# All dense f32r products as pairs of 64-row matmuls, spread one turn at a time between the score stages

## The reference

```python
xn = _layernorm(x)                                   # x: (16, 1024, 256), eps 1e-5
Q, K, V = xn @ Wq.T + bq, xn @ Wk.T + bk, xn @ Wv.T + bv   # 16 heads of 16
Q, K = _rope(Q, pos), _rope(K, pos)
scores = where(causal, einsum('bhqd,bhkd->bhqk', Q, K) / 4, -1e9)
attn = einsum('bhqk,bhkd->bhqd', softmax(scores), V)
attn_out = concat(attn) @ Wo.T + bo
h = square(relu(xn @ W_fc.T))                        # 256 -> 1024
y = h @ W_proj.T                                     # 1024 -> 256
spikes = 5 steps of a leaky integrate-and-fire neuron driven by y, counted / 5
out = x + attn_out + spikes
```

## Time and profile before

| | before |
|---|---|
| median of 3 runs | 2248.03 us |
| the runs | 2238.79, 2248.03, 2248.32 us |
| span of the profiled execution | 2243.2 us |
| the profiled execution's own time | not listed apart; its span is already above the lowest run |
| granted TensorE clock, mean | 0.987 |
| PE, PEld busy | 96%, 63% |
| DVE, ACT, POOL busy | 64%, 64%, 49% |

### The profile page before, as it was taken

One profiled execution on the slowest core, in us unless ns is written; L12 is line 12 of the kernel. 1 busy time (PEld: TensorE's weight loads), 2 busy tenths in 40 slices (PEclk: granted clock), 3 DMA queues, 4 the chain that ended last, 5 costly groups with the idle time before them and its releaser, 6 DMA issues.

```text
span 2243.2 us, 48570 instructions
## 1 busy us (share of the span) xinstructions
PE 2156.2 (96%) x16276; PEld 1406.2 (63%) x16276; DVE 1441.2 (64%) x2134; ACT 1437.5 (64%) x1673; POOL 1097.5 (49%) x1074
## 2 busy tenths in 40 slices
PE   3799999999999999999999999999999999989995
PEld 2656666666666666666666666666666666656653
DVE  5646566766757676566757667676676757646543
ACT  2376766667576675766667576665757667666663
POOL 4455454554645455453545545455464545535431
PEclk9899999999999999999999999999999999999998
DMA  3352544536345353644536354453634635345433
GB/s 137 110 175 88 157 130 115 182 87 197 101 127 168 97 184 88 173 115 132 174 84 192 101 143 144 113 185 84 188 106 120 181 91 181 92 133 155 109 97 94
DMA packets 169785, 298.89 MB, mean 133 GB/s; under 512 B 25089, under 2 KB 114945, under 8 KB 157185
## 3 DMA queue, kind: packets, MB, share of 16 engines
q1 hardware_dynamic: 169600, 296.10, 45.8%
HBM read 174.89 MB, written 103.28 MB: 124 GB/s over the span
## 4 chain that ended last, share of the span: by engine, by line
PE 83%; DVE 6%; ACT 4%; issue 4%; DMA 1%; POOL 1%; SPq 0%; ACTq 0%; DVEq 0%; POOLq 0%
PE pair L1068 33%; PE pair L1264 20%; PE pair L1228 15%; PE pair L1247 15%; ACT probs L708 2%; DVE count L928 2%; DVE stats L792 1%; ACT xT_hi L673 1%; PE pair L1155 1%; DVE h_sq L913 1%; DVE denom L852 1%; ACT h_sq L699 1%; PE pair L1080 1%; DVE numer L951 1%; POOL rot L599 0%
## 5 line engine op out<-in xcount | busy, mean ns | idle before, releaser
L708 ACT ACTIVATE probs<-pair 128x1024 f32<-128x1024 f32 x1152 | 1117.9, 1026 | 490.3 <-PE pair L1247 482.8
L617 POOL TENSOR_SCALAR_AFFINE_SELECT probs<-probs 128x512 f32<-128x512 f32 x512 | 375.0, 752 | 484.8 <-ACT probs L708 484.8
L609 POOL TENSOR_TENSOR h_lo<-h_sq,h_hi 128x512 fp32r<-128x512 f32 x256 | 383.9, 1500 | 437.4 <-DVE h_hi L915 436.9
L1264 PE MATMUL pair<-probs,v_sb 128*17 128x512 f32 (+3 forms) x6144 | 546.9, 489 | 6.1 <-DVE numer L951 5.2
L1247 PE MATMUL pair<-q_ring,k_ring 64*128 64x512 f32 (+3 forms) x3072 | 440.7, 381 | 16.8 <-ACT probs L708 13.7
L913 DVE TENSOR_TENSOR h_sq<-h_sq 128x512 f32<-128x512 f32 x256 | 201.3, 786 | 352.2 <-ACT h_sq L699 352.2
L1247 PEld LDWEIGHTS pair<-q_ring,k_ring 64*128 64x128 f32 x3072 | 227.3, 185 | 272.6 <-ACT probs L708 172.7
L1264 PEld LDWEIGHTS pair<-probs,v_sb 128*17 128x17 f32 x6144 | 152.3, 97 | 297.7 <-issue 264.1
L928 DVE SCALAR_TENSOR_TENSOR count<-y_sb,count 128x512 bf16<-128x512 f32 x256 | 294.1, 1149 | 6.8
L1228 PE MATMUL pair<-wproj_hi,h_hi 128*128 128x256 f32 x1024 | 293.0, 286 | 1.3 <-POOL h_lo L609 1.3
L1228 PE MATMUL pair<-wproj_lo,h_hi 128*128 128x256 f32 x1024 | 289.6, 283 | 0.0
(11 more groups left out here) (89 smaller groups left out, 2592.4 us busy)
## 6 DMA issues: line engine op xcount, KB each, us to landing
q_ring<-qk_dram SPq DMA_DIRECT2D x384, 128.0 KB
k_ring<-qk_dram SPq DMA_DIRECT2D x384, 128.0 KB
qk_dram<-planes SPq DMA_DIRECT2D x64, 512.0 KB, 2.8
qk_dram<-rot_b SPq DMA_DIRECT2D x64, 512.0 KB, 3.9
xn<-in_x SPq DMA_DIRECT2D x17, 1024.0 KB, 7.0
rs<-in_x SPq DMA_DIRECT2D x64, 256.0 KB, 2.7
acc_dram<-rs SPq DMA_DIRECT2D x64, 256.0 KB, 4.5
attn<-numer SPq DMA_DIRECT2D x256, 64.0 KB, 2.3
```

The lines of the kernel that those rows point to most:

```text
L609: pool.tensor_tensor(h_lo[i % HB][:, :], h_sq[i % HB][:, :], h_hi[i % HB][:, :].bitcast(F32), ALU.subtract).then_inc(h_lo_done, 1)
L617: ins = pool.affine_select(view, view, [[0, 4], [1, P]], ALU.is_ge, 0.0, base=0, channel_multiplier=-1)
L708: act.activation(probs[BUFFER[n]][:, 2 * pr:2 * pr + 2, :], pair[m % NSLOT][:, :, :], ACT.Exp, scale=SCALE).then_inc(exp_done, 1)
L1264: ins = pe.matmul(pv_bank[32 * i:32 * i + VW, q0 - g * G:G], v_sb[:, kt, 4 * quad + i, :], probs[BUFFER[n]][:, i, at:at + width(kt, g)], s ...
```

## The change

1. **Pairs.** Each dense product is issued as 64-row matmuls in pairs, one on each row half. A product is thus done in two *turns*: in turn 0 it uses the rows of one half, in turn 1 those of the other. `query_key` pairs its even and odd halves (6 pairs of 512 columns a turn); `values` pairs two token groups, or a group with a contraction carried over from the interval before; `expand` and `contract` are paired with each other (12 pairs of 256 columns a turn): the expansion of item i runs beside the contraction of item i-2.
2. **Items.** An item is now 256 features of 256 tokens; there are 16 as before. Expansion has two PSUM banks, y has one, Q/K uses the two expansion banks, and so do the values. Y is copied four times an interval instead of two times two banks.
3. **Places.** A step has five places. Score stages stand at 0, 1, 3 and 4; at 2 stand the weigh run, norms, transposes and output. After each score stage the tables `VALUES_AT`, `QK_AT` and `MLP_AT` put at most one turn, or none. An interval has 6 value turns, 8 Q/K turns and 30 MLP turns. ACT, DVE and POOL follow the same places.
4. **Moves.** Transposes go from steps 1 and 2 to 2 and 3, output from steps 3-6 to 4-7, norms from step 7 to step 8 (into `pair0`, so the stage of step 8, place 3 waits for DVE's last read, `shift_used`). On SP `store_out` goes to steps 5-8 and `store_planes` from 4-7 to 5-8, each behind what stood at step 5: `load_ring(b, d, 2, ...)`. `gather(b, 0)` goes from step 6 to 8. Spikes are issued one DVE instruction a place.

```diff
-V_AT = {0: (0, 1)}
-V_EARLY = {1: (2, 3)}
-T_AT = {1: (0, 1, 2), 2: (3,)}
-QK_AT = {2: ((0, 0), (0, 1)), 3: ((1, 0), (1, 1)), 4: ((2, 0), (2, 1)), 5: ((3, 0), (3, 1))}
-O_AT = {3: 0, 4: 1, 5: 2, 6: 3}
-NORM_AT = 7
+PLACES = 5
+VALUES_AT = {(0, 0): (0, 0), (0, 3): (0, 1), (0, 4): (1, 0), (1, 0): (1, 1), (1, 3): (2, 0), (1, 4): (2, 1)}
+TAKE_V_AT = {(0, 3): (0,), (1, 0): (1,), (1, 4): (2, 3)}
+T_AT = {2: (0, 1, 2), 3: (3,)}
+QK_AT = {(2, 4): (0, 0), (3, 0): (0, 1), (3, 4): (1, 0), (4, 0): (1, 1), (4, 4): (2, 0), (5, 0): (2, 1),
+         (5, 4): (3, 0), (6, 0): (3, 1)}
+ROTATE_AT = {at: u for at, (u, turn) in QK_AT.items() if turn}
+PLANE_AT = {(4, 0): 0, (5, 0): 1, (6, 0): 2, (7, 0): 3}
+LOW_QK_AT = {(4, 3): 0, (5, 3): 1, (6, 3): 2, (7, 3): 3}
+O_AT = {4: 0, 5: 1, 6: 2, 7: 3}
+NORM_AT = 8
+MLP_AT = {(6, 4): (0,), (7, 0): (1,), (8, 0): (2,), (8, 2): (3, 4), (9, 0): (5,), (9, 3): (6,), (9, 4): (7,),
+          (10, 0): (8,), (10, 1): (9,), (10, 4): (10,), (11, 0): (11,), (11, 3): (12,), (11, 4): (13,),
+          (12, 0): (14,), (12, 3): (15,), (12, 4): (16,), (13, 0): (17,), (13, 3): (18,), (13, 4): (19,),
+          (14, 0): (20,), (14, 3): (21,), (15, 0): (22,), (15, 3): (23,), (15, 4): (24,),
+          (16, 0): (25,), (16, 3): (26,), (16, 4): (27,), (17, 0): (28,), (17, 3): (29,)}
+Y_AT = {(10, 1): 0, (13, 0): 1, (16, 0): 2}
...
-        fc_bank, proj_bank = bank_a, (bank_b, bank_c)
+        proj_bank, fc_bank = pair[2][:, 1, :], (pair[3][:, 0, :], pair[3][:, 1, :])
+        qk_bank = fc_bank
+        norm_bank, first_norm_bank = pair[0][:, 0, :], pair[1][:, 0, :]
...
 # SP
-                    if more and n == 4:
-                        store_planes(nb, nd, 0)
-                    if last and n in (4, 5):
-                        store_out(b - 1, d - 1, n - 4)
-                    if more and n == 5:
-                        store_planes(nb, nd, 1)
                     if att and n == 5:
                         load_ring(b, d, 2, b * 2 * NUNIT + 2 * NU)
+                    if last and n in (5, 6, 7, 8):
+                        store_out(b - 1, d - 1, n - 5)
+                    if more and n in (5, 6, 7, 8):
+                        store_planes(nb, nd, n - 5)
...
 # PE
+            def query_key(nb, u, turn, tb):
+                if turn:
+                    pe.wait_ge(qk_turn, nb * 4 + u + 1)
+                elif u == 0:
+                    pe.wait_ge(xT_lo_done, tb * 4 + 3)
+                else:
+                    pe.wait_ge(rot_done, nb * 4 + u)
...
+                for n, (w, x, k) in enumerate(terms):
+                    for eo in range(2):
+                        rows = half_rows(eo + turn)
...
+            def expand_part(i, turn, n):
+                g, f, k, term = i // ITEMS_OF_GROUP, 2 * (i % ITEMS_OF_GROUP) + n // 6, n // 3 % KD, n % 3
+                rows, m, a = half_rows(i + turn), slice(f * P, (f + 1) * P), n // 6
+                w, x = ((wfc_hi, xT_hi), (wfc_lo, xT_hi), (wfc_hi, xT_lo))[term]
+                return pe.matmul(fc_bank[i % 2][:, a * T2:(a + 1) * T2], w[rows, k, m], x[rows, k, g * T2:(g + 1) * T2], ...)
...
+            def await_contract(item, i, turn, out=None, copied=None):
+                if turn:
+                    pe.wait_ge(proj_turn, item + i + 1)
+                    return
...
+                if copied is not None and i % ITEMS_OF_GROUP == 0:
+                    pe.wait_ge(y_copied, copied + i // ITEMS_OF_GROUP)
+                pe.wait_ge(h_lo_done, item + i + 1)
...
+            def expand_and_contract(nb, item, i, j, turn, out, copied, first, final):
+                await_expand(nb, item, i, turn, first, final)
+                await_contract(item, j, turn, out, copied)
+                for n in range(PART):
+                    h, y = expand_part(i, turn, n), contract_part(j, turn, n)
+                h.then_inc(fc_ps if turn else fc_turn, 1)
+                y.then_inc(proj_done if turn else proj_turn, 1)
...
+                for at in ((n, place) for n in range(NSTEP) for place in range(PLACES)):
+                    if att and place != 2:
+                        scores(b, 2 * n + place // 3, place % 3, last, more)
+                    if att and place == 2 and n in RUN_AT:
+                        run(b, RUN_AT[n], last)
...
+                    if more and at in QK_AT:
+                        query_key(nb, *QK_AT[at], tb)
+                    for t in turns.get(at, ()):
+                        mlp_turn(b, nb, item, t, last, first, final, again)
```

More of the change, by code:

```diff
@@ L111 @@
[L111 to L116, removed]
@@ new lines, in interval @@
+                    if last and place == 2 and n in O_AT:
+                        finish(b - 1, O_AT[n])
+                    if more and at in LOW_QK_AT:
+                        low_qk(nb, LOW_QK_AT[at])
+                    if more and at == (NORM_AT, 2):
+                        bound(nb, first_norm_bank if first else norm_bank)
+                        if first:
+                            replicate_bias()
+                    for i in expanded.get(at, ()) if more or final else ():
+                        activate_h(item, i)
@@ L980, in interval @@
-                    if more and n in SPIKES_NEXT:
-                        a, part = SPIKES_NEXT[n]
-                        spikes(half_of(b, 0, first, final, again), (nb * 2 + again) * 2 + a, a, range(3 * part, 3 * part + 3),
-                               nb * 4 + a + 1)
+                    if final and at in SPIKES_FINAL:
+                        a = SPIKES_FINAL[at]
+                        for s in range(STEPS + 1):
+                            spikes(half_of(b, 1, first, final, again), B * 4 + a, a, s)
@@ L1000, in interval @@
-                    for u, eo in QK_AT.get(n, ()) if more else ():
-                        rotate(nb, u, eo, items_before(b, again) if att else None)
-                    if last and n in O_AT:
-                        finish(b - 1, O_AT[n], final_bank if final else o_bank)
-                    if more and n == NORM_AT and not first:
-                        bound(nb, norm_bank)
-                    if (more or final) and n in expand_early:
-                        activate_h(item, expand_early[n])
@@ L1017, in interval @@
-                    if more and not first and n == Y1_AT or final and n == Y_FINAL_AT:
-                        take_y(half_of(b, 1, first, final, again), item + NFC - 1)
-                    if first and n == 12:
+                    if first and at == (12, 4):
                         whole_bias()
@@ new lines, in mlp_turn @@
+            def mlp_turn(b, nb, item, t, last, first, final, again):
+                i0, end, k, turn = NFT if final else 0, NFT if first else NFC, t // 2, t % 2
+                if k == 0:
+                    if first and turn == 0:
+                        pe.wait_ge(w_lo[2], 1)
+                    expand_together(nb, item, i0, turn, first, final)
+                elif i0 + k + 1 < end:
+                    if first and t == 2:
+                        pe.wait_ge(w_lo[3], 1)
+                    out = (b - 1) * 4 + 4 if last and k == 1 else None
+                    copied = copies_before(b, again) - (NTG // 2 if final else 0) if not first else 0 if k > 1 else None
+                    expand_and_contract(nb, item, i0 + k + 1, i0 + k - 1, turn, out, copied, first, final)
+                else:
+                    contract_alone(item, i0 + k - 1, turn)
@@ L1311, in interval @@
[L1311 to L1317 removed]
+                    if more and at == (NORM_AT, 2):
+                        if att:
+                            pe.wait_ge(exp_done, b * 2 * NUNIT + NORM_PAIR - NSLOT + 1)
+                        norms(nb, first_norm_bank if first else norm_bank)
@@ new lines, in interval @@
+                    for m in T_AT.get(n, ()) if place == 2 and (more or final) else ():
+                        transpose(b, tb, m, att, again)
+                    if last and place == 2 and n in O_AT:
+                        output(b - 1, O_AT[n])
+                    if att and at in values_at:
+                        m, turn = values_at[at]
+                        if carried and m < CARRIED:
+                            values_and_contract(b, m, turn, again)
+                        else:
+                            values_together(b, m, turn, again)
```

550 lines of the change are left out of this document (271 added, 279 removed).

## The result

The changed kernel takes 2436.28 us (median of 4 runs, 2427.05 to 2439.31), the kernel before 2244.84 us beside it (4 runs): ratio 1.085, 95% interval 1.082 to 1.089. I had forecast 2313 us, and 2370 as the upper end: slower was right, the size was off by almost a factor of three.

A forecast was written before the change was run, and what follows sets the result against it. PE was taken as the bound, busy 133.2 of 133.5 us an interval. 133.5 - 6.9 (tiling changes) + 10.9 (waits) = 137.5 us; +60 us for 15 intervals and +5 for the first on 2248 gave 2313 us, range 2205 to 2370.

The forecast's parts named there:

- turn 1 close behind turn 0: PE wait for turn 0's last matmul before loading, 0.13 us each, 11 times: 1.4 us an interval; bounds 0 and 0.23.
- Changes of tiling: Tiling changes on PE fall from 73 to 38 an interval, about 0.20 us each: 6.9 us removed.
- Streaming: Matmul streaming unchanged: pairs of 256 columns 0.12 us apart, a turn 1.43 us, a Q/K turn 1.37.
- Step 5, place 4: PE waits 3.6 us at a Q/K turn for a rotation whose store lands late behind 13 ring DMAs.
- Step 6, place 4: PE waits 1.9 us at the first MLP turn for the rotation, store landing and odd half.
- waits do not hold PE: Rival: long landing waits and gaps between turns covered, 4.0 us of waits remain, 130.6 us an interval, 2210 us; chance 0.26.
- The issue bound: Rival: dense matmul issue makes pairs 5% slower, 2.6 us an interval more, 2352 us; chance 0.09.
- Step 2, place 4: PE waits 1.2 us at a Q/K turn for high and low parts of three blocks after the transposes.
- Steps 8 and 9, place 0: PE waits 1.0 us each for exp, as three score stages follow each other with two PSUM pairs.
- The h chain just covered: ReLU to remainder gets over 5 us of cover, taken as no wait; if not, 1 to 3 us more.
- The first interval, +5: The first interval, without score stages as cover, takes 5 us more.
- The changes remain: Rival: row halves with other operands still empty the array, so the 6.9 us stay, 2417 us; chance 0.05.

The follow-up runs named there:

- e2: e1 with the four bias adds on POOL moved from iteration 13 place 4 to iteration 14 place 4; 2321.48 us, ratio 1.037.
- e3: e2 with every dense product on the whole 128-row array again, same places and queue orders; 2481.17 us, ratio 1.107.
- b1: The kernel before, with SP's third-part ring loads put ahead of the first Q/K plane's store, old tilings kept; 2342.46 us, ratio 1.044.
- e1: The changed kernel with SP's third-part ring loads put back behind the first and second Q/K plane stores; 2365.02 us, ratio 1.056.
- e5: e2 with four MLP turns moved: the first two, the fifth, and turn 23 to ahead of a weigh run; 2311.48 us, ratio 1.031.
- e7: e5 with exp on half its columns, middle spike comparisons on 64 of 512, masks on one head of four; 2285.55 us, ratio 1.019.
- c1: e2 with both turns of each MLP product together, 15 blocks instead of 30 spread turns; 2457.54 us, ratio 1.095.
- e6: e5 with the second MLP turn moved to iteration 7 place 4 and the third to iteration 8 place 2; 2287.36 us, ratio 1.020.

## Why the prediction was wrong, point by point

My interval was 133.5 - 6.9 + 10.9 = 137.5 us; it is 145.8, 8.3 more. The 1.4 us for turn 1 close behind turn 0, which I had booked as a wait, is an open load, and the account above counts it as PE's own time. So I had own time fall by 5.5 us (6.9 - 1.4) and waits rise by 9.5. At full clock own time fell by 3.0 (2.5 us missing), the slow clock added 3.0, and stands rose by 12.2 (2.7 more; the weigh run of step 15 alone is 2.85). That is 8.2 us.

- **Changes of tiling, 6.9 us removed: the count right, the gain too large by 2.5 us.** 612 groups are 38 an interval, as counted. But PE's own time falls by 3.0 us only (133.1 to 130.1, read in e2, where the clock is full). By kind: scores -3.0, MLP and values together -0.8, output with its own change +0.6. The failed step is to take the whole "about 0.20 us" of a change, the step at the boundary and the open load behind it, as gone with the change. e3 bears the 0.20 out only where nothing else holds the load; on the average it is 0.15, because in the pairs' version a load stays open where a turn waits on a semaphore. "I am fairly sure of this term" stood over the one that carried the rival of a gain.
- **Streaming: right a pair (0.12 us), wrong a turn.** 1.48 against 1.43, Q/K 1.47 against 1.37, for the open first load. Over the 44 turns of an interval it is 2.3 us (64.7 of own time against 62.4), nearly all of the 2.5 missing above. The issue bound is out: pairs hold 0.12 through whole turns. The rule of the Trainium skill that I cited, "TensorE: Matmul & The Clock Gate", section "Wait — 56ns, not 53.3ns?", would make a pair 0.124 us. The trace shows 0.117 to 0.121, so it does not bound this kernel; whether hardware decoding was off, as the rule asks, no run shows.
- **Step 5, place 4: mechanism and place right, 3.6 us against 4.8.** The landing took 5.0 us and not 3.9. b1 shows that I had also read its cover wrongly: even the old kernel stands with this order.
- **Step 6, place 4: 1.9 us against none**, since the longer wait ahead of it gave DVE its time; it is there (1.1 us) once that one is gone (e1, e2). I had added two waits that lie one behind the other on the same chain. The landing in this chain has a second waiter that I had not walked, ACT's ReLU (iteration 8, place 1: about 1 us in e1, e2, e5 and e7).
- **Step 2, place 4: 1.2 against 1.17. Steps 8 and 9, place 0: 1.0 each against 1.05 and 1.07. Step 10, place 4: 0.5 against 0.49. Step 1, place 3: 0.3 against 0.44.** The short chains, walked from rows, came out almost to the digit.
- **Turn 1 close behind turn 0:** with a score stage between, it shows only as the open load, 0.18 us a product (0.34 + 1.51 against 0.23 + 1.44) where I had 0.13; without one it is 0.30 to 0.34 us (c1), above my upper bound of 0.23.
- **"The h chain just covered": true of h, false of what shares its queue.** The missing step is the weigh run of step 15, 2.85 us for a mask that stood on POOL behind the bias adds and a remainder of h. I had walked the places that had changed, and this run had not; what had changed was how soon PE came to it.
- **The clock: not in my sum at all.** Behind the stands of 4.8 and 2.7 us it was granted at half for some microseconds; together 3.0 us an interval (133.1 against 130.1 of own time), a quarter of the 12.2 us that an interval grew. e1 and e2 take away the stands, and the slow turns go with them, but for one in twelve intervals.
- **The first interval, +5: it is +17.6.** A stand of 6.4 us at the fourth Q/K turn is in it, the slow clock (0.93 in that interval), and turns that follow each other directly, each with the wait of c1.

Of the rivals, "waits do not hold PE" was wrong at its root. Its 2210 us counted on 126.6 us of own time and 4.0 of waits; with 130.1 the same waits make an interval of 134.1 us, a little longer than the old one. "The changes remain" (2417) has the nearest number for another reason.

In the order of their size, shown by an experiment each: SP's order (67 us, e1, and 98 in the old kernel, b1), POOL's order (44, e2), the spread's short waits (37, e5 and e6). Against them stands what the pairs save in these places, 160 us (e3 against e2), but compared with the old places only 3.0 us an interval. What stays open: how the remaining 44 us of e6 divide among the single chains; I did not try to remove the wait for `xT_lo` or the one for the landing behind ACT's ReLU, and the start and the end of the run were not studied.

## What to carry to other kernels

When PE's order is tightened, walk every queue again, not only the places that moved: a store behind 13 loads on SP, a mask behind bias adds on POOL, or a bank shared with an output product cost more here than the tiling changes gave back. Price a removed change as the difference between two kernels that differ in nothing else; the rows around one change also hold the open load, which a semaphore keeps open just as well. Count a stand of PE of some microseconds with the slow clock behind it. And where a wait is put down to exp, look at what the engine did just before: here it was a DMA's landing.

## What the runs showed of the hardware

- The granted clock fell to 0.50 in the turn right behind a stand of 4.84 us, and was back in the next turn, some 3 us later; behind one of 2.7 us in the weigh run it fell only 1.4 us after PE had gone on. In b1 the same happened behind 3.18 us with whole-row matmuls. Behind a stand of 1.86 us it fell in one of twelve intervals of e2, and behind 1.7 to 2.5 us in eleven of twelve of e3.
- Two row halves run beside each other at the full rate: pairs of 256 columns 0.12 us apart, whether the two start together or up to 0.04 us apart.
- A product that is accumulated from both row halves in turn, with a semaphore wait between, took 0.42 to 0.46 us from the last pair of the one to the first of the other (c1).
- A turn of 12 pairs whose first load waited on a semaphore took 1.51 us and the one stage ahead of it 0.34; where the load had gone out early it was 1.44 and 0.23 (e2).
- A landing of a plane's store took 5.0 us when it was issued right behind 13 ring loads.
